# The state product of a two-layer megakernel in 32 rows per sequence, on two row groups of TensorE

## The reference, cut to what matters

```
xp = h @ Wp + bp                       # 128 -> 32 state channels
h_t = sigmoid(lam) * h_(t-1) + B * xp  # scan over the 512 tokens
y  = einsum(h, C) ; out = y @ Wo + bo  # 32 -> 128
z  = out + h_in ; x = x + ga * LayerNorm(z)
```

## Time and profile before

| what | value |
|---|---|
| three runs, us | 536.96, 538.70, 538.67 |
| median, us | 538.67 |
| span of the profiled execution, us | 534.6 |
| TensorE (PE) busy, us and share of the span | 507.4, 95% |
| VectorE busy | 388.8, 73% |
| ScalarE busy | 327.2, 61% |
| GpSimd busy | 170.4, 32% |

### The profile page before, as it was taken

One profiled execution on the slowest core, in us unless ns is written; L12 is line 12 of the kernel. 1 busy time (PEld: TensorE's weight loads), 2 busy tenths in 40 slices (PEclk: granted clock), 3 DMA queues, 4 the chain that ended last, 5 costly groups with the idle time before them and its releaser, 6 DMA issues.

```text
span 534.6 us, 9257 instructions
## 1 busy us (share of the span) xinstructions
PE 507.4 (95%) x3304; PEld 392.7 (73%) x3304; DVE 388.8 (73%) x1020; ACT 327.2 (61%) x599; POOL 170.4 (32%) x241
## 2 busy tenths in 40 slices
PE   8599989998999999989899999999999989999995
PEld 6568877786687878868567777767677668888884
DVE  6986987698768785646989888887979864554433
ACT  4978968686867788846364454646454444555541
POOL 3510640033003002101425254534536364343311
PEclk9869999999999999998999999999999999999998
DMA  8500000000003000004343332323333100000101
GB/s 307 176 1 1 2 0 1 1 2 1 0 1 121 22 2 0 2 0 159 112 147 101 130 113 80 110 83 110 103 113 116 50 1 2 21 21 23 38 20 40
DMA packets 18607, 31.15 MB, mean 58 GB/s; under 512 B 2400, under 2 KB 13152, under 8 KB 18432
## 3 DMA queue, kind: packets, MB, share of 16 engines
q1 hardware_dynamic: 17504, 30.00, 17.4%
q10 hardware_dynamic: 1056, 0.52, 0.3%
HBM read 28.19 MB, written 2.33 MB: 57 GB/s over the span
## 4 chain that ended last, share of the span: by engine, by line
PE 46%; ACT 3%; DMA 2%; DVE 1%; SPq 1%; issue 1%; POOL 1%; POOLq 0%; ACTq 0%
PE bank L1929 10%; PE bank L2010 6%; PE bank L165 5%; PE bank L167 5%; PE bank L166 5%; PE bank L1941 3%; PE bank L1975 3%; PE bank L1963 2%; PE bank L241 2%; PE bank L2002 1%; PE bank L1950 1%; ACT att_qT L1766 1%; DMA cum_rows<-att_cum 1%; PE bank L2018 1%; ACT h_hi L247 1%; DMA att_prob<-cut_rows 1%
## 5 line engine op out<-in xcount | busy, mean ns | idle before, releaser
L1066 PE MATMUL bank<-ffn_g_hi,w_hi 128*128 128x512 f32 x288 | 116.7, 405 | 0.1
L1067 PE MATMUL bank<-ffn_g_lo,w_hi 128*128 128x512 f32 x288 | 114.0, 396 | 0.0
L607 DVE TENSOR_TENSOR ffn_g_lo<-ffn_full,ffn_g_hi 128x512 fp32r<-128x512 f32 x96 | 67.1, 699 | 27.2 <-ACT ffn_full L853 25.8
L1414 DVE TENSOR_TENSOR_SCAN att_prob<-att_prob,bank 128x512 f32<-128x512 f32 x64 | 77.0, 1208 | 7.5 <-DMA att_prob<-cut_rows 7.4
L1929 PE MATMUL bank<-att_qT,h_full 128*128 128x512 f32 x128 | 67.3, 610 | 1.3 <-DVE att_prob L1425 1.3
L1793 ACT COPY att_qT<-bank 128x512 f32<-128x512 f32 x64 | 36.6, 583 | 46.0 <-PE bank L167 43.1
L1066 PEld LDWEIGHTS bank<-ffn_g_hi,w_hi 128*128 128x128 f32 x288 | 54.3, 188 | 13.8 <-issue 1.7
L1067 PEld LDWEIGHTS bank<-ffn_g_lo,w_hi 128*128 128x128 f32 x288 | 54.3, 189 | 11.7
L853 ACT ACTIVATE ffn_full<-bank,cols 128x512 f32<-128x512 f32 x64 | 44.2, 696 | 20.8 <-PE bank L1067 14.5
L1425 DVE TENSOR_TENSOR att_prob<-bank,att_prob 128x512 f32<-128x512 f32 x64 | 43.2, 676 | 18.9 <-PE bank L1929 18.7
L1607 POOL TENSOR_TENSOR att_vw<-att_v,att_prob 128x128 f32<-128x128 f32 x64 | 26.1, 408 | 92.1 <-DVE att_prob L1414 92.1
(11 more groups left out here) (230 smaller groups left out, 1137.8 us busy)
## 6 DMA issues: line engine op xcount, KB each, us to landing
att_prob<-cut_rows SPq DMA_DIRECT2D x32, 512.0 KB, 4.7
att_wide<-cum_rows SPq DMA_DIRECT2D x64, 48.0 KB, 1.9
out<-att_vw SPq DMA_DIRECT2D x7, 256.0 KB, 2.3
x<-in_x SPq DMA_DIRECT2D x3, 512.0 KB, 12.1
w_raw<-in_w_all SPq DMA_DIRECT2D x1, 1152.0 KB, 8.4
w_raw<-in_w_all SPq DMA_DIRECT2D x1, 768.0 KB, 9.6
v_raw<-in_v_all SPq DMA_DIRECT2D x1, 576.0 KB, 5.9
x<-in_x ACTq DMA_DIRECT2D x2, 256.0 KB, 3.5
```

The source lines that it names most:

```text
L607: dve.tensor_tensor(lo, full[j % 4][:, :], hi.bitcast(F32), ALU.subtract).then_inc(low, 1)
L1066: pe.matmul(acc, w[0], x[0], start=start, stop=False)
L1067: return pe.matmul(acc, w[0], x[1], start=False, stop=stop)
L1414: dve.tensor_tensor_scan(w, w, eyes[:, :], 0.0, ALU.mult, ALU.add).then_inc(decay_ready, 1)
```

## The change

The state product contracts over the 32 rows of its own sequence instead of over 128 rows. For that, `state` shrinks to 64 partitions and `cw` to one tile of 64 rows and 128 columns; the three clearing instructions on GpSimd go, and the two copies that fill `cw` become one. In `z` all four identity products come first, then the wait for the scan, then the four state products. In the loop a new function `z_pair` follows tile j = 8 and does both sequences: it claims both banks, issues the eight identity products, waits for the scan, and then issues the state products of the two sequences in turn, one on rows 0 to 31 and the other on rows 32 to 63. Nothing follows tile j = 9 any more. PE instructions stay the same in number.

```diff
-            for name, shape in (("out", [P, T, D]), ("hT", [P, S]), ("state", [P, S]), ("zn", [P, T, D])):
+            for name, shape in (("out", [P, T, D]), ("hT", [P, S]), ("state", [2 * SD, S]), ("zn", [P, T, D])):
...
-        cw = sb("cw", [P, SLOTS, D])
+        cw = sb("cw", [STRIPS, D])
...
-                    if i < 3 and j in (8, 9):
-                        uses.append((("z", 2 * i + 2 + j - 8), 4 + j - 8))
+                    if i < 3 and j == 8:
+                        uses += [(("z", 2 * i + 2 + s), 4 + s) for s in range(SLOTS)]
...
-                    dve.wait_ge(cleared, 3)
-                    for s in slots:
-                        at = slice(s * SD, (s + 1) * SD)
-                        dve.tensor_copy(cw[at, s, :], bank("cw", 0)[at, 0:D]).then_inc(cw_ready, 1)
+                    dve.tensor_copy(cw[:, :], bank("cw", 0)[0:STRIPS, 0:D]).then_inc(cw_ready, 1)
...
-                for s in slots:
-                    pool.memset(state[s][:, :], 0.0).then_inc(cleared, 1)
-                pool.memset(cw[:, :, :], 0.0).then_inc(cleared, 1)
...
+                def skip(ps, s, t):
+
+                    c = slice(t * P, (t + 1) * P)
+                    pe.matmul(ps[:, c], hT[s][:, c], r["ident"][:, :], start=t == 0, stop=False, skip_group_check=True)
+
+                def through(ps, p, s, t):
+
+                    c, strip = slice(t * P, (t + 1) * P), slice(s * SD, (s + 1) * SD)
+                    return pe.matmul(ps[:, c], state[p % 2][strip, c], cw[strip, :], start=False, stop=True, skip_group_check=True)
+
                 def z(claim, b):
                     p, s = b // 2, b % 2
-                    pe.wait_ge(scanned, p + 1)
                     ps = claim(pe, "z", b)
                     for t in range(T):
-                        c = slice(t * P, (t + 1) * P)
-                        pe.matmul(ps[:, c], hT[s][:, c], r["ident"][:, :], start=True, stop=False)
-                        ins = pe.matmul(ps[:, c], state[p % 2][:, c], cw[:, s, :], start=False, stop=True)
+                        skip(ps, s, t)
+                    pe.wait_ge(scanned, p + 1)
+                    for t in range(T):
+                        ins = through(ps, p, s, t)
                     ins.then_inc(mm, 1)
+
+                def z_pair(claim, p):
+                    ps = [claim(pe, "z", 2 * p + s) for s in slots]
+                    for s in slots:
+                        for t in range(T):
+                            skip(ps[s], s, t)
+                    pe.wait_ge(scanned, p + 1)
+                    for t in range(T):
+                        for s in slots:
+                            ins = through(ps[s], p, s, t)
+                            if t == T - 1:
+                                ins.then_inc(mm, 1)
...
-                            if i < 3 and j in (8, 9):
-                                z(claim, e + j - 8)
+                            if i < 3 and j == 8:
+                                z_pair(claim, i + 1)
```

More of the change, by code:

```diff
@@ L326, in front @@
         loaded_keep, loaded_qk, loaded_l1 = sem("loaded_keep"), sem("loaded_qk"), sem("loaded_l1")
-        ones_set, cleared, cw_ready, silu_ready, lam_ready = sem("ones_set"), sem("cleared"), sem("cw_ready"), sem("silu_ready"), sem("lam_ready")
+        ones_set, cw_ready, silu_ready, lam_ready = sem("ones_set"), sem("cw_ready"), sem("silu_ready"), sem("lam_ready")
         mm = sem("front_mm")
@@ L422, in __call__ @@
                     signal, count = {
-                        "mod": lambda k: (mod_ready, (4, 8)[k]), "flip": lambda b: (h_ready, b + 1), "cw": lambda k: (cw_ready, 2),
+                        "mod": lambda k: (mod_ready, (4, 8)[k]), "flip": lambda b: (h_ready, b + 1), "cw": lambda k: (cw_ready, 1),
                         "gap": lambda k: (gap_ready, 1), "u": lambda p: (u_ready, p + 1), "z": lambda b: (znormed, b - 1) if b >= SLOTS else (centred, b + 1),
@@ L552, in scan @@
                     dve.wait_ge(u_ready, p + 1)
-                    dve.tensor_tensor_scan(state[p % 2][0:STRIPS, :], lam_col[:, 0:1].broadcast_to([STRIPS, S]), u[:, :], 0.0, ALU.mult, ALU.add).then_inc(scanned, 1)
+                    dve.tensor_tensor_scan(state[p % 2][:, :], lam_col[:, 0:1].broadcast_to([STRIPS, S]), u[:, :], 0.0, ALU.mult, ALU.add).then_inc(scanned, 1)
                 def centre(b):
@@ L1048, in prepare @@
                         spread(claim, k)
-                    pe.wait_ge(cw_ready, 2)
+                    pe.wait_ge(cw_ready, 1)
                     z(claim, 0)
```

## The result

The kernel after takes 539.43 us (median of 19 runs, 537.24 to 542.11); the kernel before, run beside it, takes 537.45 us (19 runs, 535.76 to 540.53). The ratio is 1.004, with a 95% interval of 1.0027 to 1.0054. So the change costs 2 us, 1.4 to 2.9 by the interval. At 0.4% it stays under the 0.5% that the forecast took as its bound, though the interval's upper end lies just above it. The profiled execution has a span of 536.1 us, against 534.6.

A forecast was written before the change was run, and what follows sets the result against it. TensorE, busy for 95% of the span, was taken as the bound. Start +0.3, i = 0 -0.5, i = 1 and 2 +0.34 each sum to +0.5 us: about 539.1 where the median is 538.7, range 537.2 to 542.0.

The forecast's parts named there:

- the case (within 0.5%): Whole kernel: no change that can be told, 536.0 to 541.4 us; chance of this case 0.62, its own range 538.0 to 540.6.
- Overlap of the row groups: State products of a z pair on TensorE: two row groups run at once, 16 instructions in 0.88 us instead of 1.79.
- no overlap: Rival, chance 0.17: row groups' weight loads go one after another, state products stay at 1.79 us; +3.2 us, 541.9.
- a drain at every hand-over: Rival, chance 0.04: every alternating state product pays 0.10 plus an exposed 0.11 us; +13 in all, 552.
- Change of shape: TensorE around each group of state products: entering and leaving cost 0.4 us a visit, bounds 0 and 0.6.
- the third rival: Rival, chance 0.13: changing shape is free for row groups, visits give back 0.4 us each; -1.3 us, 537.3.
- The wait for bank 5: Pairs i = 1 and 2: TensorE stands still 0.85 us until VectorE's add (line 586) has read the bank.
- "Nothing is added" behind tile 11: Pairs i = 1 and 2: statistics end 0.3 us late at lower(10), but ScalarE's queue sets the pace, so no further cost.
- i = 0: First loop pair: bank 5 is free, identity products cover the scan wait, VectorE's pace from lower(10) counts; -0.5 us.
- Start: z(0) and z(1): four changes of shape +0.8, identity products ahead of the scan -0.5; +0.3 us reaches the chain.
- fourth rival: Rival, chance 0.04: the half-clock stretch, 22.0 to 35.7 us, ends elsewhere, moving the time 1 to 2 us either way.
- The 4.0 us around it: Time around the profiled span of 534.6 us, taken as unchanged and added to the forecast span of 535.1.

The follow-up runs named there:

- e4: Kernel after, but the two z issued one by one behind tiles 8 and 9, so no row groups alternate; 539.49 us, ratio to before 1.0041.
- e2: Kernel after, but the odd sequence's z of pairs i = 1 and 2 lies in bank 7, so no wait for bank 5; 537.85 us, ratio to before 1.0003.
- e5: Kernel after, but VectorE takes both z statistics (moments_out) one tile earlier; 537.71 us, ratio to before 0.9995.
- e6: Kernel after with both edits: odd z of pairs 1 and 2 in bank 7, statistics one tile earlier; 535.25 us, ratio to before 0.9963.
- e7: e6, but the start also does its two z's as an alternating pair; 535.30 us, ratio to before 0.995.
- e9: e6's order, banks and statistics, but state products over 128 zero-padded rows; 535.79 us, ratio to before 0.9981.
- e3: Kernel after's order and wait, but state products over 128 zero-padded rows, with the clears and both cw copies; 540.63 us, ratio to before 1.0053.

## Why the prediction was right, and where it wasn't

The sign came out and the case (within 0.5%), with the sum too small: +0.5 forecast, +1.4 found in layer 0, +2.0 measured. That the time is met to 0.3 us (539.1 forecast, 539.43 measured) is luck. The forecast started from 538.67, the median of three runs, where 19 runs give 537.45; this 1.2 too much covers most of the 1.5 that the sum lacks. And the change can be told: over 19 runs each the interval of the ratio, 1.0027 to 1.0054, leaves out 1.

**Overlap of the row groups: right, to 0.01.** Forecast were 0.88 us of rounds for the sixteen instructions. The rows of the kernel after have 1.09 with the first load (0.11) and leaving (0.10), and eight instructions of one row group in e4 take the same 1.09. The estimate from the Trainium skill's speedup for four row groups ("TensorE: Matmul & The Clock Gate", Part 3), 1.16 us, would make it 1.37, which no row shows. The rivals of no overlap and of a drain at every hand-over are out.

**Change of shape: right.** The 0.4 a visit was read off column tiles, and e4 confirms it for row tiles: two visits a pair cost 0.80. The rule of the Trainium skill that a change of tiling mode drains TensorE ("TensorEngine Tiling (Array Packing)", Key Properties) agrees, and 0.2 on each side, 0.1 of it an exposed load, is its price here. Free of charge, the third rival, it is not.

**The wait for bank 5: right in place and releaser, too small.** Forecast 0.85, measured 1.02 and 1.01 (e2). The forecast stopped at VectorE's end plus 0.05. VectorE's add starts at 97.02 and takes 0.67; TensorE starts 0.15 after its end (97.69 to 97.84), and the identity products behind the wait take 0.09 longer, because their first weight load was not done ahead.

**"Nothing is added" behind tile 11: wrong.** This is the step that failed. The prediction had `lower(10)` late by 0.3 and put ScalarE's queue ahead of it, but it didn't follow the statistics one engine further. GpSimd makes the shift from them, and ScalarE's own queue waits for the shift: +0.36 in i = 1 and again in i = 2 (e5). The two terms together (0.17 and 0.36) make +0.89 and +0.91 out of +0.34, to 0.04.

**i = 0: right.** -0.5 forecast, -0.57 measured. `lower(10)` starts at 52.36, right behind the statistics, as the prediction had it, and 1.1 sooner than in the earlier trace rows. This comparison holds against the stretch's start, which is 0.55 sooner itself, so 0.55 remain. What I hadn't seen is the `lower` held for 1.1 us at the same place in before (58.64 for 1.79); it was there to be read.

**Start: nearly right.** +0.3 forecast, +0.2 measured at ScalarE. z(0) starts 0.56 sooner (13.77 instead of 14.33) and TensorE reaches the flag's products 0.13 later (20.11 instead of 19.98), so the four changes of shape cost 0.7 there, not 0.8. VectorE's flag instruction comes at 20.49 instead of 20.35.

**The stretch at the half clock (fourth rival): it did end elsewhere.** It ended 4.1 us sooner in the profiled execution than in the earlier trace rows:

```profile
21.40:31.60 10.20, 5.32 (x13) 3.20 (x14) 8.61 (x44) 5.93 (x11) 4.67 (x4) 0.50 0.02 4
256.90:260.30 3.40, 3.40 (x14) 2.90 (x13) 3.40 (x5) 1.12 (x2) 1.51 (x3) 0.50 0.38 84
```

and layer 1 has a second one, at 256.9. In before this second one lies at 240.5, with the same length. Both stand elsewhere again in the profiled executions of other kernels of this study, so the profiled spans alone couldn't have told the 2 us. From the first feed-forward activation to the start of stretch a the kernel after takes 15.61 us and before 16.36, so in this pair of executions the clock gave 0.75 back. The medians don't rest on it: the mean granted clock is 0.9812 over the 19 runs of the kernel after and 0.9815 over the 78 of before beside the experiments.

**"The 4.0 us around it": a wrong reading.** That figure was the median of three runs less the span of one shorter, profiled execution. Over all runs the time around the span of the same run is 2.1 us for before and 2.35 for after. It changed nothing in the +0.5, but it carried the 1.2 us named above into the time.

**What stays open.** Of the measured 2.0 us, 1.4 lies in layer 0 and about 0.3 around the span. The remaining 0.3 is within the interval of the ratio. Layer 1 is not accounted for: in the profiled executions it takes 298.4 us in the kernel after and 297.6 before (from the start of the last row of stretch c to the end of the span), and whether the change has a part in that or only the other place of its half-clock stretch, no run tells. For other kernels the stretches and the ratio agree only to about 1 us (e2: stretches -0.8, ratio +0.2); against the mean spans, which leave out the time around, stretches and start agree to 0.7 (e2: -0.6 and +0.1). So the table is good for differences inside layer 0, not for totals.

## What to carry to other kernels

In this kernel a product on part of the rows paid 0.4 us of shape changes a visit, alone or alternating. So gather such products and alternate the row groups: one group by itself gained nothing over zero-padded rows (e4). When a product moves ahead, look up who frees its bank at the new time, and then follow its result through every engine that works on it, not only the next: here two small waits of 1.0 and 0.36 us cost 1.4 us in each of two pairs, where the row groups gained 0.5. With both waits taken away the version is 0.995 to 0.996 of the kernel before (e6, e7), where the change as made was 1.004. Part of that is not the change's own: the statistics' new place gives 1.1 us in stretch a with or without row groups, and without them the version is 0.998 (e9).

## What the runs showed of the hardware

- Two row groups of 128 weight columns worked fully at once, weight loads included: 16 instructions in eight rounds of 0.11 us, 1.09 us in all, where e3's one-by-one products take 1.71.
- A VectorE instruction with two inputs in SBUF took 1.78 instead of 0.68 us beside a GpSimd add, one with a single input (line 487) 1.18 instead of 0.17; a GpSimd add took 1.75 instead of 1.29 and a GpSimd inverse root 1.39 instead of 1.02 beside such a two-input VectorE instruction. A shift of the schedule by a tile removed the one or made the other.
- The time around the span varies between runs of one kernel (1.97 to 2.54 us in the kernel after, 2.04 to 2.14 in before), and its mean between kernels, from 1.9 us (e4) to 2.4 us (e7), with no cause that a trace shows.
